# An attention and mixture-of-experts layer on one core: in the last stage, the weightings of loaded rows move one chunk ahead

## What is computed

```python
x = _layernorm(x + attn(x, Wq, bq, Wk, bk, Wv, bv, Wo, bo))    # 16 heads of 8, window 32
logits = x @ gate_w                                            # 8 experts
top_w, top_idx = jax.lax.top_k(logits, 2)
top_w = softmax(top_w)
y = gelu(x @ w1[e] + b1[e]) @ w2[e] + b2[e]                    # for the two chosen e
x = _layernorm(x + top_w[0] * y[first] + top_w[1] * y[second])
```

## Time and profile before

| what | us |
|---|---|
| median of 3 runs | 759.72 (759.15 to 766.87) |
| the profiled execution, whole | 757.98 |
| its span in the trace | 756.2 |
| last stage: first load issued, first multiplication begun | 696.70, 700.66 |
| last stage: end of the last sum, end of the span | 748.89, 756.2 |

### The profile page before, as it was taken

The page is one execution under the profiler, slowest core; times in us unless marked ns, Lnnn a source line. Parts: engine busy times, 40 slices in busy tenths (PEclk is TensorE's granted clock), DMA queues, the critical chain, the costliest instruction groups (busy, mean ns, idle before and its releaser), DMA issues.

```text
span 756.2 us, 26507 instructions
## 1 busy us (share of the span) xinstructions
PE 605.1 (80%) x10228; PEld 436.7 (58%) x10228; DVE 505.0 (67%) x1574; ACT 391.3 (52%) x935; POOL 349.7 (46%) x364
## 2 busy tenths in 40 slices
PE   5889988888887888877772598888888888884895
PEld 3556655555555655544551487777777777783332
DVE  8668767767777757755647477667767676762664
ACT  3556645555655655534330464565555555552476
POOL 9101334434434434354436055554555555665574
PEclk9999999999999999968875699999999999997898
DMA  3986666776766666644212676666666666641794
GB/s 95 129 169 139 160 138 138 153 127 123 145 140 146 143 113 130 134 96 98 64 57 71 222 259 212 220 233 209 236 205 238 208 235 209 229 144 35 254 273 120
DMA packets 126818, 121.90 MB, mean 161 GB/s; under 512 B 46865, under 2 KB 105300, under 8 KB 126694
## 3 DMA queue, kind: packets, MB, share of 16 engines
q1 hardware_dynamic: 116374, 102.28, 52.0%
q0 software_dynamic: 8640, 17.06, 7.8%
q10 hardware_dynamic: 1680, 0.87, 0.5%
HBM read 40.68 MB, written 28.12 MB: 91 GB/s over the span
## 4 chain that ended last, share of the span: by engine, by line
PE 66%; issue 16%; DVE 5%; POOL 4%; DMA 3%; ACT 2%; SPq 2%; another core or an unknown queue 1%; ACTq 0%; POOLq 0%; DVEq 0%
PE pO L1367 13%; PE pT L1254 8%; PE pO L1273 8%; PE pT L1353 6%; PE pS L1353 6%; PE pS L1244 5%; PE pS L1260 4%; PE pC L1205 3%; PE pM L1284 2%; POOL area L654 2%; POOL area L660 2%; PE pC L1173 1%; DVE nmax L892 1%; PE pC L1174 1%; DMA xT<-xT_in_dram 1%
## 5 line engine op out<-in xcount | busy, mean ns | idle before, releaser
L645 POOL DMA_INDIRECT zs<-PT,dst x142 | 148.0, 1042 | 131.4 <-ACT PT L794 97.2
L621 POOL DMA_INDIRECT xs<-Y,pos x128 | 126.0, 984 | 172.5 <-PE pS L1244 124.1
L1367 PE MATMUL pO<-area,Q 128*128 128x128 f16 x1704 | 120.1, 220 | 28.5 <-issue 27.7
L734 ACT COPY PT<-pT 128x512 f32<-128x512 f32 x128 | 74.9, 586 | 104.7 <-PE pT L1254 98.5
L1367 PEld LDWEIGHTS pO<-area,Q 128*128 128x128 f16 x1704 | 103.0, 98 | 39.3 <-issue 37.5
L1273 PEld LDWEIGHTS pO<-VB,PT 128*32 128x32 f32 x4096 | 58.5, 114 | 79.8 <-issue 76.4
L1273 PE MATMUL pO<-VB,PT 128*32 128x18 f32 x4096 | 79.3, 190 | 30.7 <-issue 27.8
L892 DVE TENSOR_REDUCE nmax<-pS 128x8 bf16<-128x512 f32 x128 | 87.4, 683 | 7.8 <-PE pS L1244 7.6
L1254 PE MATMUL pT<-ident,E 128*128 128x128 f32 x512 | 89.7, 301 | 0.0
L1130 DVE SCALAR_TENSOR_TENSOR Q<-VB,Q 128x1024 f16<-128x1024 f32 x71 | 87.0, 1225 | 2.4
L1128 DVE TENSOR_SCALAR Q<-VB 128x1024 f16<-128x1024 f32 x71 | 54.2, 763 | 48.9 <-ACT VB L805 46.1
(11 more groups left out here) (201 smaller groups left out, 1091.0 us busy)
## 6 DMA issues: line engine op xcount, KB each, us to landing
area<-wall SPq DMA_DIRECT2D x71, 546.0 KB
E<-xs SPq DMA_DIRECT2D x71, 132.0 KB
VB<-vwin SPq DMA_DIRECT2D x64, 144.0 KB
area<-zs SPq DMA_DIRECT2D x16, 512.0 KB, 4.3
area<-k_nat SPq DMA_DIRECT2D x90, 64.0 KB
Q<-q_nat SPq DMA_DIRECT2D x45, 128.0 KB
vwin<-v_nat SPq DMA_DIRECT2D x32, 144.0 KB
xT<-xT_in_dram SPq DMA_DIRECT2D x16, 256.0 KB
```

The source lines that it names most:

```text
L621: nc.gpsimd.indirect_dma_start(xs, bass.IndirectOffsetOnAxis(ap=pos[:, c, t:t + 1], axis=0), Y[:, t, 0:ROW], None).then_inc(rows_out[t % B ...
L645: nc.gpsimd.indirect_dma_start(zs, bass.IndirectOffsetOnAxis(ap=dst[:, u, n:n + 1], axis=0), zrow[:, v, n, :], None, bounds_check=TOPK * T ...
L1367: last = nc.tensor.matmul(o, hp[:, v, c, n * P:(n + 1) * P], wts2[:, part, c, :], start=False, stop=(c == FC - 1 and part == 0 and hp is Hl))
```

## The change

GpSimd's loop runs one round longer. The multiplication of c now stands before the power of c - 2 instead of c - 1. ScalarE's loop also runs one round longer, and its weighting of c stands before the outputs of c - 3 instead of c - 2. No instruction is added or removed, no wait is dropped, and buffers and their counts stay the same.

```diff
-            for c in range(CHUNKS + 1):
+            for c in range(CHUNKS + 2):
                 if in_chunks(c):
...
                     nc.gpsimd.tensor_tensor(zin[:, u, 1, :, :], zin[:, u, 1, :, :], view(wts[:, c * CH:(c + 1) * CH, 1], [[TOPK, CH], [0, D]]),
                                             ALU.mult).then_inc(z1_done, 1)
-                g = c - 1
+                g = c - 2
                 if in_chunks(g):
                     reach(pool, var2_done, g + 1)
...
-            for c in range(CHUNKS + 2):
+            for c in range(CHUNKS + 3):
                 if in_chunks(c):
...
-                g = c - 2
+                g = c - 3
                 if in_chunks(g):
                     w, v = g % YBUFS, g % MBUFS
                     reach(act, nmr2_done, g + 1)
```

## The result

The changed kernel takes 757.66 us (median of 20 runs, 752.85 to 760.32) against 760.36 us for the kernel before (median of 20, 758.01 to 766.87). The ratio is 0.9937, with a 95% interval of 0.9915 to 0.9959: about 0.6% faster, which is clear of noise and still inside the 1% that I called no change. The profiled execution took 754.42 us, with a span of 752.6.

The account below looks back on a forecast made before the run. A ring of waits through GpSimd, TensorE and VectorE was taken as the last stage's bound. 13 rounds x (2.887 - 2.580) = 4.0 us, taken as 3.9, off the 759.72 us median gave 755.8 us, range 753.3 to 759.8.

Parts of the forecast that it names:

- The likeliest case: Last stage: pace falls to 2.58 to 2.62 us per chunk, median 755.8 us; chance 0.80.
- The ring sets the pace, and it opens: Last stage: GpSimd's power and multiplication, two matmuls, VectorE's statistics and offset take 5.73 us for two chunks, then for three.
- TensorE's 2.58 us is next: Last stage: once GpSimd's waits open, TensorE's three matmuls per chunk set the pace at 2.58 us.
- The third rival: Last stage: another ring of the same length sets the pace, so nothing is gained; 759.7 us, chance 0.05.
- ScalarE's half at nothing: Last stage: moving ScalarE's weighting saves nothing, since its own loop of waits, 2.45 us per chunk, wasn't the bound.
- The cover: Last stage: margin of 0.13 us per chunk between ScalarE's loop at 2.45 us and TensorE's 2.58.
- 13 rounds, 3.9 us: Last stage: 13 rounds at 2.580 instead of 2.887 us save 4.0 us; at 2.59, 3.9, which was taken.
- The start and the tail stay: Last stage: sums 0 to 2 and the 7.3 us after the last sum were to stay unchanged.
- Transfers at nothing: Last stage: loads and stores were to cost nothing, the last load landing just in time near 739.9.
- rival 1: Last stage: transfers become the bound at 2.69 us per chunk, saving only 2.6 us; 757.1 us, chance 0.09 with other in-between paces.
- The second rival: Last stage: multiplications hold up VectorE's L1143, its round becoming 3.05 us and losing 2.1 us; 761.8 us, chance 0.03.
- The median: Whole kernel: the saving taken off the earlier median of 759.72 us gives 755.8 us, 0.5% less.

Follow-up runs that it names:

- The version in which VectorE adds: Against the changed kernel, VectorE adds the token's own row for two of four tiles while weighting, relieving TensorE; 639.39 and 743.05 us, 0.9904 and 0.9864 of the kernel before.

## Why the prediction was right

The likeliest case came true by its own steps.

- *The ring sets the pace, and it opens.* Shown from two sides: without L1375 the kernel before keeps its pace (5.79 us for two chunks), and the changed kernel doesn't (2.197).
- *TensorE's 2.58 us is next.* 2.575 in every round, TensorE busy for 28 of 28 us, and a still longer lead gives nothing. The third rival, no gain, falls with it.
- *ScalarE's half at nothing.* Shown by the two halves: 2.575 with GpSimd's alone, no change of pace with ScalarE's alone. The cover that I put at 0.13 us per chunk was enough, and it is thin: with GpSimd's half alone the weighting ended 0.39 us before its L1380.
- *13 rounds, 3.9 us.* It was 4.06. The difference is the pace, 2.575 for 2.58 to 2.59.
- *The start and the tail stay.* The tail does (8.29 and 8.33 us). The start varies with the clock, see below; I had taken it for fixed, and the 0.63 us that it gave in the profiled execution are not the change's. That the span came out at 752.6 for the 752.3 forecast is in part luck, since 1.13 us more ahead of the stage and 0.63 us less at its start nearly cancel.
- *Transfers at nothing.* No load was waited for after the fourth, and rival 1 falls with it. But the limit in the first rival was mis-sized: I took 292 GB/s from 263 GB/s at a share of 0.90. The version in which VectorE adds moved 305 GB/s at 0.94, and the changed kernel without L1375 moved 331 GB/s over 22 us at a share of 1.02. A share below 1 didn't mean that the transfers were near their limit.
- *The second rival.* Its mechanism is real (1.26 for 0.47 us), its place was rightly excluded (L1143 kept its 0.47), and its price was too high: 2.67 us for VectorE's round instead of 3.05, and none at all for the whole in this short stage. The Trainium skill (SBUF — State Buffer, "SBUF: two separate sides") says, of VectorE's instructions in a two-port mode or with two inputs in SBUF, that the one that comes second blocks for the whole instruction of the first. The pair that ends with the multiplication agrees. The pair beside a power doesn't: it keeps its 0.47 us (721.12) while the power runs for 1.05 (721.21). Why the power holds nothing up stays open.
- *The median.* 755.8 was forecast from a median of three runs; with twenty the kernel before is at 760.36, and the change measures 0.63% (0.41 to 0.85) by the ratio and 0.36% by the medians, against 0.5% forecast. The changed kernel's 757.66 is 1.9 us above the 755.8.

## What to carry to other kernels

When the chain of waits alternates between two instructions of an engine that also idles, look for the ring that closes over the program order of that engine: its length divided by the number of items it carries is the pace, and moving an independent instruction one item ahead raises the divisor without removing any work. What it can give ends at the busiest engine's own time, and it is paid in buffers: with six it was free, with four it cost more than it gave. Only behind such an opening does an edit that relieves the busiest engine pay, and the same edit inside the ring makes things worse.

## What the runs showed of the hardware that I hadn't expected

**Chips differ outside this stage.** The version in which VectorE adds took 743.05 us on one chip and 639.39 us on another, with the same pace of 2.209 us in the last stage. Each chip was used at its own time, so that the chip itself is the cause is argued and not shown. Two groups of TensorE on the slower chip (L1368 is the experts' second product, L1274 attention's values; busy, mean ns | idle before, what ended it):

```profile
L1368 PE MATMUL pO<-area,Q 128*128 128x128 f16 x1704 | 122.6, 220 | 30.1 <-issue 29.1
L1274 PE MATMUL pO<-VB,PT 128*32 128x18 f32 x4096 | 77.8, 190 | 31.6 <-issue 29.5
```

The same on the faster chip:

```profile
L1368 PE MATMUL pO<-area,Q 128*128 128x128 f16 x1704 | 110.6, 219 | 0.0
L1274 PE MATMUL pO<-VB,PT 128*32 128x18 f32 x4096 | 63.2, 189 | 15.0 <-issue 12.1 <-DMA VB<-vwin 2.3 <-ACT PT L734 0.2
```

A matmul takes the same time, but on the slower chip TensorE idles for "issue", that is for nothing that the profile shows, in the many small matmuls, 29.1 us before L1368 alone where the other has none. Busy and idle time together, the two groups make up some 73 of the 99 us between the spans (740.3 and 641.2). In the last stage, with 48 long matmuls in a row, nothing of it is seen. What TensorE waits for in the other two stays open; it wasn't tried.

**The clock at the start of the stage.** From L1380 of chunk 0 to that of chunk 1 it was 4.04 us in the kernel before, 3.41 in the changed kernel, 3.95 in the changed kernel once more, and 3.1 to 4.0 in the experiments that leave TensorE its three matmuls and don't touch this stretch. TensorE comes to the stage after idling for the first loads, at a granted clock of 0.50 (1.2 GHz). In the kernel before its first matmul is at 701.85 and the clock is 1.00 (2.4 GHz) from 706.90 on; in the changed kernel these are 702.98 and 706.60. So it rose 5.05 us after the first matmul in the one and 3.62 us in the other. By the spread from 3.1 to 4.0 the moment at which it rises is worth up to 0.9 us here, a fifth of the whole saving.
